# A vision block on one core: layer norm writes the padded layout, clearings move to the start, VectorE masks the turned keys, the last q and k pair is projected behind the first scores

## The chip, the cores and the metric

The kernel runs on one NeuronCore of a Trainium2 chip. The metric is the device time of one launch in microseconds (us). The engines are TensorE (PE, its weight loads PEld), VectorE (DVE), ScalarE (ACT), GpSimd (POOL) and SyncE (SP), which here issues the DMAs. Each runs its own instructions in order; semaphores join them.

## The reference

16 images of 36 patches and a class token (S = 37 rows of D = 256) go through quantised patch embedding, attention and an expert layer:

```
h = tok(x)                       # rms norm, 8-bit activations, ternary weights, + class token, position
h = h + attn(layernorm(h))
h = h + ffn(layernorm(h))

# attn: 16 heads of 16; q_rot, k_rot are q, k turned by position
num  = exp(q_rot @ k_rot^T * scale)
den  = sum(exp(q @ k^T * scale))          # of the unturned q, k
attn = where(causal, num / den, 0)
y    = (attn @ v) @ Wout + bout
# ffn: softmax attention in 8 heads of 64, values and outputs through the expert that the gate picks
```

## The kernel before, in words

**Embedding.** Rows come in six groups (`G`) of three images (111 rows; the sixth group has one image). Each group is squared and rounded by ScalarE, scaled and clipped by VectorE, turned and multiplied by TensorE. GpSimd computes `rrms`, a power of -1/2, from ScalarE's sums. The ternary weights come from `tw`, whose absolute sum VectorE takes (L864) once its DMA has landed.

**First layer norm.** `embed(g)` and `ln_stats` on VectorE, `rstd_of` on GpSimd, `ln_apply` on VectorE (L836, writes `xhat`), `turn_x` on TensorE (L1175). ScalarE's `x1_hi` (L562) then takes the high part of the turned group from PSUM, and VectorE's `x1_lo` (L852) the rest: each fp32 product is made of three matmuls on such halves (`split3`, L267 to L269). Both write tokens without gaps, `x1hi` and `x1lo` [128, 2, 666].

**Projections.** `PJ` lists twelve jobs, in pairs: q and k of images 0 to 7 for each of two chunks of 128 columns (jobs 0 to 3), v of images 0 to 7 (4, 5), q and k of images 8 to 15, chunk 0 (6, 7), v of the others (8, 9), q and k of images 8 to 15, chunk 1 (10, 11). A q or k job is 6 matmuls of 296 columns, a v job 12 of 256. `PJB` names each job's PSUM bank; `bank_free` waits until ScalarE, and for q and k VectorE, have read the job that last used it. The v jobs take their stationary operand from a second, padded copy, 64 columns an image, whose 27 spare columns are zero: `x1hi2`, `x1lo2`, written by ScalarE in `x1_apart` (L638, four instructions).

**Reads of the projections.** ScalarE copies each q or k job twice under a mask of heads (L587, `qun`, `kun`) and each v job in four pieces into `vblk` (L596). VectorE's `rope(r)`, r = 0 to 3, turns a q and k pair in five steps (L922 to L925, then two masked copies L927 into `qrot`); ScalarE's `keys_turned(r)` (L663) writes the turned keys into `krot` with two masked copies. `rope_t` counts VectorE's steps, `krot_ready` ScalarE's. GpSimd clears `vblk` and the spare columns of `kun` and `krot` behind the last `rstd_of` (L467, L469), then adds a bias to `h` (L472) once `x1lo` is complete.

**Attention.** Four blocks (`b`) of four images. On TensorE: `scores(b, 0)` (turned), `denominators(b - 1)`, `scores(b, 1)` (unturned), `attend(b)`; scores are L1254, `attend` L1272, denominators L1284. ScalarE takes the exponentials (L654), VectorE applies the causal mask (L934, `causal`), the reciprocal and the product (L948, L953). Then come the output projection (L1297), the second layer norm, gates, value experts and output experts, which the change does not touch. The order on every engine is that in which its code is written.

## Time and profile before

| what | us |
|---|---|
| median of 3 runs | 263.17 |
| lowest, highest | 259.93, 264.06 |
| time of the profiled execution | 263.35 |
| its span | 260.8 |
| TensorE busy | 222.7 (85%) |
| VectorE busy | 181.9 (70%) |
| ScalarE busy | 99.8 (38%) |
| GpSimd busy | 79.1 (30%) |

The span runs from the first to the last instruction; 2.55 us of the execution's time lie around it. The busy shares are averages over stages with different limits: TensorE's 40 slices are full (8 or 9 tenths) in most of the span, and emptiest in the first 11 and around the fifteenth to seventeenth. The granted clock of TensorE, in the line PEclk, stands at half its full 2.4 GHz in some slices between 39 and 98 us. The stretch of the change ends where attention is in its regular step, at about 69 us.

### The profile page before, as it was taken

How to read it: one execution, taken by the hardware profiler on the slowest of the kernel's cores; microseconds unless marked ns; L12 is line 12 of the kernel's file. 1: busy time of each engine (PE TensorE's matmuls, PEld its weight loads, DVE VectorE, ACT ScalarE, POOL GpSimd, SP SyncE). 2: the span in 40 equal slices, each digit the busy share in tenths (PEclk: the TensorE clock that was granted, in tenths of full speed). 3: DMA queues.
4: the chain of work that ended last, by engine and by line, in shares of the span. 5: the costliest groups of instructions: out<-in, count | busy, mean ns of one | idle time of the engine just before them, and what ended most of it. 6: DMA issues, size and time to landing. Idle time of an engine off the chain costs nothing.

```text
span 260.8 us, 5163 instructions
## 1 busy us (share of the span) xinstructions
PE 222.7 (85%) x2079; PEld 192.4 (74%) x2079; DVE 181.9 (70%) x316; ACT 99.8 (38%) x196; POOL 79.1 (30%) x82
## 2 busy tenths in 40 slices
PE   0146845977899996999999999999999999999994
PEld 0026735966788865899766777777898999999993
DVE  2678995935556268679343766866579997979982
ACT  3677636698544213254444126235520211120000
POOL 4153887200023205240031653775666000000000
PEclk9999995696555579799999999999999999999999
DMA  6995000000000000200034100604700542461102
GB/s 183 252 324 218 1 3 0 1 0 3 3 3 0 3 3 0 80 4 0 0 96 161 64 21 1 230 14 148 200 3 26 188 152 86 154 188 48 48 0 94
DMA packets 7181, 19.56 MB, mean 75 GB/s; under 512 B 1043, under 2 KB 1878, under 8 KB 7030
## 3 DMA queue, kind: packets, MB, share of 16 engines
q1 hardware_dynamic: 7158, 19.24, 23.0%
q8 instruction: 16, 0.26, 0.4%
q14 instruction: 7, 0.06, 0.1%
HBM read 18.55 MB, written 0.68 MB: 74 GB/s over the span
## 4 chain that ended last, share of the span: by engine, by line
PE 48%; DVE 27%; ACT 9%; issue 8%; POOL 4%; DMA 3%; SPq 0%; DVEq 0%; ACTq 0%; POOLq 0%
PE ps L267 10%; PE ps L269 9%; PE ps L268 9%; DVE gx L1119 7%; PE ps L1254 7%; DMA tw<-tok_weight 3%; DVE xhat L836 3%; PE ps L1297 3%; ACT vblk L596 2%; PE ps L1454 2%; DVE oelo L1093 2%; PE ps L1272 1%; DVE amax L796 1%; DVE stat L825 1%; PE ps L1284 1%
## 5 line engine op out<-in xcount | busy, mean ns | idle before, releaser
L1119 DVE TENSOR_TENSOR gx<-maskb,oT 128x1184 fp32r<-128x1184 bf16 x31 | 42.3, 1411 | 0.6 <-PE ps L269 0.5
L267 PE MATMUL ps<-gx,oelo 128*128 128x296 f32 x124 | 37.8, 304 | 0.6 <-DVE gx L1119 0.6
L1056 DVE COPY_PREDICATED v<-onehot,ps 128x512 f32<-128x512 uint8 (+3 forms) x40 | 25.7, 660 | 17.6 <-PE ps L269 17.3
L269 PE MATMUL ps<-gx,oehi 128*128 128x296 f32 x124 | 37.2, 300 | 0.0
L268 PE MATMUL ps<-gx,oehi 128*128 128x296 f32 x124 | 37.0, 298 | 0.0
L267 PE MATMUL ps<-vehi,x2lo 128*128 128x512 f32 (+3 forms) x90 | 35.2, 392 | 0.0
L268 PE MATMUL ps<-velo,x2hi 128*128 128x512 f32 (+3 forms) x90 | 33.3, 370 | 0.0
L269 PE MATMUL ps<-vehi,x2hi 128*128 128x512 f32 (+3 forms) x90 | 33.2, 369 | 0.0
L486 POOL TENSOR_TENSOR velo<-veraw,vehi 128x1024 fp32r<-128x1024 f32 x8 | 19.1, 2389 | 23.4 <-ACT vehi L680 17.3
L267 PEld LDWEIGHTS ps<-gx,oelo 128*128 128x128 f32 x124 | 23.3, 188 | 1.8 <-issue 1.4
L268 PEld LDWEIGHTS ps<-gx,oehi 128*128 128x128 f32 x124 | 23.4, 188 | 0.0
L269 PEld LDWEIGHTS ps<-gx,oehi 128*128 128x128 f32 x124 | 23.3, 188 | 0.0
L1155 PE MATMUL ps<-ident_bf,qb 111*128 111x111 bf16 x36 | 4.5, 297 | 17.4 <-DVE qb L821 17.3
L267 PEld LDWEIGHTS ps<-vehi,x2lo 128*128 128x128 f32 (+1 forms) x90 | 16.2, 180 | 4.2 <-issue 0.7
L269 PEld LDWEIGHTS ps<-vehi,x2hi 128*128 128x128 f32 (+1 forms) x90 | 16.2, 180 | 3.7
L268 PEld LDWEIGHTS ps<-velo,x2hi 128*128 128x128 f32 (+1 forms) x90 | 16.2, 181 | 2.8
L1155 PEld LDWEIGHTS ps<-ident_bf,qb 111*128 111x128 bf16 x36 | 3.1, 139 | 19.3 <-DVE qb L821 19.2
L750 ACT ACTIVATE oehi<-oeraw 128x1024 fp32r<-128x1024 f32 x8 | 8.5, 1065 | 18.8 <-DMA oeraw<-output_w 18.8
L449 POOL TENSOR_TENSOR w2lo<-w2raw,w2hi 128x544 fp32r<-128x544 f32 x4 | 5.3, 1333 | 34.1 <-DVE en L934 33.1
L1254 PE MATMUL ps<-qrot,krot 64*101 64x74 f32 x128 | 12.0, 379 | 3.3 <-ACT vblk L596 3.3
L454 POOL TENSOR_TENSOR rstd<-lnv,half_neg 111x1 f32<-111x1 f32 x12 | 7.9, 658 | 22.9 <-DVE lnv L827 22.8
L1254 PEld LDWEIGHTS ps<-qrot,krot 64*101 64x101 f32 x128 | 11.2, 285 | 3.8 <-issue 3.6
(167 smaller groups left out, 508.4 us busy)
## 6 DMA issues: line engine op xcount, KB each, us to landing
maskb<-mask_rows SPq DMA_DIRECT2D x32, 148.0 KB, 3.7
veraw<-value_w SPq DMA_DIRECT2D x8, 512.0 KB, 3.8
oeraw<-output_w SPq DMA_DIRECT2D x8, 512.0 KB, 3.6
...
```

What stands on the lines that cost most here:

```text
L267: pe.matmul(o, llo, rhi, start=start, stop=False)
L268: pe.matmul(o, lhi, rlo, start=False, stop=False)
L269: return pe.matmul(o, lhi, rhi, start=False, stop=stop)
L454: pool.tensor_tensor(rstd[:, which, g:g + 1], lnv[:, which, g:g + 1], half_neg[0:R, 0:1], ALU.pow).then_inc(sm["rstd_ready"], 1)
L486: pool.tensor_tensor(velo[:, e % NVR], veraw[:, e % NVR], vehi[:, e % NVR].bitcast(F32), ALU.subtract).then_inc(sm["velo_ready"], 1)
L750: act.activation(oehi[u % NOR][:], oeraw[RAW[u]][:], ACT.Copy).then_inc(sm["oehi_ready"], 1)
L836: dve.tensor_scalar(xhat[:, g % 2], h[:, g], mv[:, which, g, 0:1], rstd[:, which, g:g + 1], ALU.subtract, ALU.mult).then_inc(sm["xhat_read ...
L1056: dve.copy_predicated(v2[0:m, t, h0:h1], bcast(onehot[0:m, t, h0:h1, e], 2, DH2), ps[0:m, JBANK[n], 0:(h1 - h0) * DH2].rearrange("p (a b) ...
L1119: dve.tensor_tensor(gx[:, k % NGR].rearrange("p a b t -> p a (b t)"), bcast(maskb[:, w % NMR, k % MEU], 1, 2), oT[:, c % 2].bitcast(F32), ...
L1155: ins = pe.transpose(dst[:, c * (R + 1):c * (R + 1) + R], qb[:, g % NQB, c * P:(c + 1) * P], ident_bf[0:R, 0:R])
L1254: ins = pe.matmul(ps[0:QR, 2 * t + r, o:o + JS * S], key, qry, start=True, stop=True)
L1297: ins = pe.matmul(ps[0:R, o, w:w + D], yT[:, k, g * R:(g + 1) * R], wo[:, k], start=(k == 0), stop=(k == KC - 1))
```

## The change

There is no second copy of x1: ScalarE and VectorE write `x1hi` and `x1lo` in the padded layout [128, 2, 16, 64], and the q and k jobs read 38 columns of each image (`SE`, of which the last is a cleared one), so 304 columns a matmul instead of 296. `x1_apart` is gone. The clearings of `vblk` and `kun` stand first on GpSimd, that of `krot` and of `ones` behind group 0's `rrms`, those of `x1hi` and `x1lo` behind group 1's; `vblk`, `kun`, `krot` and the exponentials get memory that no earlier buffer uses. VectorE writes `krot` itself, two instructions more in each `rope` (`RSTEPS` 8), and `keys_turned` is gone. Jobs 10 and 11, their reads on ScalarE and `rope(3)` on VectorE move behind the first scores, and the v jobs 8 and 9 use banks 4 and 5.

```diff
 NPATCH = SIDE * SIDE
...
 HALF = T // 2
+QH = B // 2 * SE
...
-        x1hi = sbuf(proj, "x1hi", [P, KC, TP], F32R, "right")
-        x1lo = sbuf(proj, "x1lo", [P, KC, TP], F32R, "right")
-        x1hi2 = sbuf(proj, "x1hi2", [P, KC, B, DH2], F32R, "right")
-        x1lo2 = sbuf(proj, "x1lo2", [P, KC, B, DH2], F32R, "right")
+        x1hi = sbuf(proj, "x1hi", [P, KC, B, DH2], F32R, "right")
+        x1lo = sbuf(proj, "x1lo", [P, KC, B, DH2], F32R, "right")
         wo = sbuf(first, "wo", [P, KC, D])
         biasb = sbuf(first, "biasb", [R, 2, D])
+        kun = sbuf(first, "kun", [P, KC, B, QR])
+        krot = sbuf(first, "krot", [P, KC, B, QR])
+        w2raw = sbuf(first, "w2raw", [P, KC, W2C])
+        vblk = sbuf(first, "vblk", [QR, B, PAIRS, 2, DH1])
...
+        ropet = sbuf(first, "ropet", [P, 2, 2, QH])
+        ropex = sbuf(first, "ropex", [P, 2, QH])
+        partner = sbuf(first, "partner", [P, 2, QH])
...
+        rden = sbuf(proj, "rden", [P, UN * S], F32, "right")
+        yT = sbuf(proj, "yT", [P, KC, TP], F32, "right")
+        en = sbuf(proj, "en", [QR, 2, 2, RT, KC, 2, JS, S], F32, "right")
+        ed = sbuf(proj, "ed", [QR, RT, KC, BI, JS, S], F32, "right")
...
-        PJB = [0, 1] + [2, 3] + [4, 5] + [6, 7] + [0, 1] + [4, 5]
+        PJB = [0, 1] + [2, 3] + [4, 5] + [6, 7] + [4, 5] + [6, 7]
         PJPREV = [max([m for m in range(n) if PJB[m] == PJB[n]], default=-1) for n in range(NPJ)]
-        RSTEPS = 6
+        RSTEPS = 8
...
-            pool.memset(ones[:], 1.0).then_inc(sm["pool_setup"], 1)
             pool.memset(half_neg[:], -0.5).then_inc(sm["pool_setup"], 1)
-            for apart in (x1hi2, x1lo2):
-                pool.memset(apart[:, :, :, S:].bitcast(F32), 0.0).then_inc(sm["apart_zero"], 1)
-            pool.wait_ge(sm["pool_setup"], 2)
+            pool.memset(vblk[:].rearrange("p i h a b -> p (i h a b)"), 0.0).then_inc(sm["vblk_zero"], 1)
+            pool.memset(kun[:, :, :, S:DH2], 0.0).then_inc(sm["keys_zero"], 1)
+            pool.wait_ge(sm["pool_setup"], 1)
 
...
+                if g == 0:
+                    pool.memset(krot[:, :, :, S:DH2], 0.0).then_inc(sm["keys_zero"], 1)
+                    pool.memset(ones[:], 1.0).then_inc(sm["pool_setup"], 1)
+                elif g == 1:
+                    for apart in (x1hi, x1lo):
+                        pool.memset(apart[:, :, :, S:].bitcast(F32), 0.0).then_inc(sm["apart_zero"], 1)
...
-            pool.wait_ge(sm["wqlo_ready"], NW)
-            pool.memset(vblk[:].rearrange("p i h a b -> p (i h a b)"), 0.0).then_inc(sm["vblk_zero"], 1)
-            for keys in (kun, krot):
-                pool.memset(keys[:, :, :, S:DH2], 0.0).then_inc(sm["keys_zero"], 1)
             pool.wait_ge(sm["x1lo_ready"], G)
...
-                act.activation(x1hi[:, :, g * R:(g + 1) * R],
-                               ps[:, 4 + g % 2, 0:KC * R].rearrange("p (c t) -> p c t", c=KC),
+                n = images(g)
+                act.activation(x1hi[:, :, g * GI:g * GI + n, 0:S],
+                               ps[:, 4 + g % 2, 0:KC * R].rearrange("p (c i s) -> p c i s", c=KC, s=S)[:, :, 0:n],
                                ACT.Copy).then_inc(sm["x1hi_ready"], 1)
...
-                    src = ps[:, PJB[n], 0:HALF].rearrange("p (i s) -> p i s", s=S)
+                    src = ps[:, PJB[n], 0:QH].rearrange("p (i s) -> p i s", s=SE)[:, :, 0:S]
...
-            def x1_apart(hf):
-                tc, im = slice(hf * HALF, (hf + 1) * HALF), slice(hf * B // 2, (hf + 1) * B // 2)
-                for once, apart in ((x1hi, x1hi2), (x1lo, x1lo2)):
-                    src = once[:, :, tc].bitcast(F32).rearrange("p c (i s) -> p c i s", s=S)
-                    act.activation(apart[:, :, im, 0:S], src, ACT.Copy).then_inc(sm["x1_apart"], 1)
...
-            def keys_turned(r):
-
-                hf, c = r // KC, r % KC
-                act.wait_ge(sm["keys_zero"], 2)
-                act.wait_ge(sm["rope_t"], RSTEPS * r + 4)
-                src = ropet[:, r % 2, 1].rearrange("p (i s) -> p i s", s=S)
-                for j in range(2):
-                    ins = act.activation(krot[:, c, hf * B // 2:(hf + 1) * B // 2, DH2 * j:DH2 * j + S], src, ACT.Copy,
-                                         scale=cols("par")[:, j:j + 1])
-                ins.then_inc(sm["krot_ready"], 1)
-
-            for n in range(NPJ):
+            for n in range(NPJ - 2):
                 proj_read(n)
-                if n == 2:
-                    x1_apart(0)
-                elif n == 4:
-                    x1_apart(1)
-                elif n in (5, 7, 9):
-                    keys_turned((n - 5) // 2)
...
-                    keys_turned(3)
+                    proj_read(NPJ - 2)
+                    proj_read(NPJ - 1)
...
-                tc = slice(g * R, (g + 1) * R)
-                dve.tensor_tensor(x1lo[:, :, tc], ps[:, 4 + g % 2, 0:KC * R].rearrange("p (c t) -> p c t", c=KC),
-                                  x1hi[:, :, tc].bitcast(F32), ALU.subtract).then_inc(sm["x1lo_ready"], 1)
+                n = images(g)
+                hi, lo = (x[:, :, g * GI:g * GI + n, 0:S] for x in (x1hi, x1lo))
+                dve.tensor_tensor(lo, ps[:, 4 + g % 2, 0:KC * R].rearrange("p (c i s) -> p c i s", c=KC, s=S)[:, :, 0:n],
+                                  hi.bitcast(F32), ALU.subtract).then_inc(sm["x1lo_ready"], 1)
...
-                own = ps[:, PJB[n]:PJB[n] + 2, 0:HALF]
+                own = ps[:, PJB[n]:PJB[n] + 2, 0:QH]
...
-                if r >= 2:
-                    dve.wait_ge(sm["krot_ready"], r - 1)
...
-                    many(dve.tensor_scalar(qrot[:, c, im, j], ropet[:, r % 2, 0].rearrange("p (i s) -> p i s", s=S),
-                                           cols("par")[:, 4 + j:5 + j], None, ALU.mult))
+                    many(dve.tensor_scalar(qrot[:, c, im, j], tmp[:, 0], cols("par")[:, 4 + j:5 + j], None, ALU.mult))
+                for j in range(2):
+                    many(dve.tensor_scalar(krot[:, c, im, DH2 * j:DH2 * j + S], tmp[:, 1], cols("par")[:, j:j + 1],
+                                           None, ALU.mult))
...
-            for r in range(2 * KC):
-                rope(r)
+            rope(0)
+            dve.wait_ge(sm["keys_zero"], 2)
+            rope(1)
+            rope(2)
             causal(0)
+            rope(3)
...
-                        wb, tc, col = kind, slice(a * HALF, (a + 1) * HALF), slice(c * P, (c + 1) * P)
-                        ins = split3(pe, ps[:, PJB[n], 0:HALF], wqhi[:, wb, k, col], wqlo[:, wb, k, col],
-                                     x1hi[:, k, tc], x1lo[:, k, tc], k == 0, k == KC - 1)
+                        wb, im, col = kind, slice(a * B // 2, (a + 1) * B // 2), slice(c * P, (c + 1) * P)
+                        ins = split3(pe, ps[:, PJB[n], 0:QH].rearrange("p (i s) -> p i s", s=SE),
+                                     wqhi[:, wb, k, col], wqlo[:, wb, k, col],
+                                     x1hi[:, k, im, 0:SE], x1lo[:, k, im, 0:SE], k == 0, k == KC - 1)
                 else:
                     pe.wait_ge(sm["apart_zero"], 2)
-                    pe.wait_ge(sm["x1_apart"], 2 * (a * NVI * 2 // B + 1))
...
-            for n in range(NSTART, NPJ):
+            for n in range(NSTART, NPJ - 2):
...
-                pe.wait_ge(sm["krot_ready"], KC * late)
                 pe.wait_ge(sm["act_read"], act_reads(PJ.index(("qk", late - 1, KC - 1, 1))))
                 if b == kind == 0:
-                    for n in range(NPJ):
-                        if PJB[n] < 4 and n not in PJPREV:
-                            bank_free(n)
+                    bank_free(NEARLY - 1)
...
+                    bank_free(NPJ - 3 if b == 0 else NPJ - 1)
...
             for b in range(NB):
                 scores(b, 0)
-                if b:
+                if b == 0:
+                    proj_job(NPJ - 2)
+                    proj_job(NPJ - 1)
+                else:
                     denominators(b - 1)
                 scores(b, 1)
```

TensorE, end of the projections and start of attention, before (the last nine matmuls of jobs 10 and 11, then scores(0, 0), scores(0, 1) and attend(0)):

```order
L267 MATMUL ps<-x1hi,wqlo 128x296
L268 MATMUL ps<-x1lo,wqhi 128x296
L269 MATMUL ps<-x1hi,wqhi 128x296
L267 MATMUL ps<-x1hi,wqlo 128x296
L268 MATMUL ps<-x1lo,wqhi 128x296
L269 MATMUL ps<-x1hi,wqhi 128x296
L267 MATMUL ps<-x1hi,wqlo 128x296
L268 MATMUL ps<-x1lo,wqhi 128x296
L269 MATMUL ps<-x1hi,wqhi 128x296
L1254 MATMUL ps<-qrot,krot 101x74 x16
L1254 MATMUL ps<-qun,kun 101x74 x16
L1272 MATMUL ps<-en,vblk 32x37 x32
```

The same place in the change (L1233 is `scores`, L1250 `attend`; the three rows ahead end job 9):

```order
L265 MATMUL ps<-wqhi,x1lo 101x256
L266 MATMUL ps<-wqlo,x1hi 101x256
L267 MATMUL ps<-wqhi,x1hi 101x256
L1233 MATMUL ps<-qrot,krot 101x74 x16
L265 MATMUL ps<-x1hi,wqlo 128x304
L266 MATMUL ps<-x1lo,wqhi 128x304
L267 MATMUL ps<-x1hi,wqhi 128x304
L265 MATMUL ps<-x1hi,wqlo 128x304
L266 MATMUL ps<-x1lo,wqhi 128x304
```

The twelve matmuls of jobs 10 and 11 now stand between scores(0, 0) and scores(0, 1).

VectorE, before: `rope(2)` from its first row, `rope(3)`, then the causal mask of block 0.

```order
L922 STREAM_SHUFFLE partner<-ps 128x592
L923 TENSOR_TENSOR ropet<-ps,cst 128x592
L924 TENSOR_TENSOR ropex<-partner,cst 128x592
L925 TENSOR_TENSOR ropet<-ropet,ropex 128x592
L927 TENSOR_SCALAR qrot<-ropet,cst 128x8x37 x2
L922 STREAM_SHUFFLE partner<-ps 128x592
L923 TENSOR_TENSOR ropet<-ps,cst 128x592
L924 TENSOR_TENSOR ropex<-partner,cst 128x592
L925 TENSOR_TENSOR ropet<-ropet,ropex 128x592
L927 TENSOR_SCALAR qrot<-ropet,cst 128x8x37 x2
L934 TENSOR_TENSOR en<-en,cst 101x592 x2
```

In the change `rope(2)` ends with two copies into `krot`, the mask comes next and `rope(3)` behind it:

```order
L899 STREAM_SHUFFLE partner<-ps 128x608
L900 TENSOR_TENSOR ropet<-ps,cst 128x16x37
L901 TENSOR_TENSOR ropex<-partner,cst 128x16x37
L902 TENSOR_TENSOR ropet<-ropet,ropex 128x16x37
L904 TENSOR_SCALAR qrot<-ropet,cst 128x8x37 x2
L906 TENSOR_SCALAR krot<-ropet,cst 128x8x37 x2
L913 TENSOR_TENSOR en<-en,cst 101x592 x2
L899 STREAM_SHUFFLE partner<-ps 128x608
L900 TENSOR_TENSOR ropet<-ps,cst 128x16x37
L901 TENSOR_TENSOR ropex<-partner,cst 128x16x37
L902 TENSOR_TENSOR ropet<-ropet,ropex 128x16x37
```

ScalarE, reads of jobs 2 to 7 before (L638 is `x1_apart`, L663 `keys_turned`):

```order
L587 ACTIVATE qun<-ps,cst 128x8x37 x2
L638 ACTIVATE x1hi<-x1hi 128x2x8x37
L638 ACTIVATE x1lo<-x1lo 128x2x8x37
L587 ACTIVATE kun<-ps,cst 128x8x37 x2
L596 ACTIVATE vblk<-ps 37x2x8x16 x4
L638 ACTIVATE x1hi<-x1hi 128x2x8x37
L638 ACTIVATE x1lo<-x1lo 128x2x8x37
L596 ACTIVATE vblk<-ps 37x2x8x16 x4
L663 ACTIVATE krot<-ropet,cst 128x8x37 x2
L587 ACTIVATE qun<-ps,cst 128x8x37 x2
L587 ACTIVATE kun<-ps,cst 128x8x37 x2
L663 ACTIVATE krot<-ropet,cst 128x8x37 x2
```

The same reads in the change, and those of jobs 8 to 11 around the exponentials:

```order
L587 ACTIVATE qun<-ps,cst 128x8x37 x2
L587 ACTIVATE kun<-ps,cst 128x8x37 x2
L596 ACTIVATE vblk<-ps 37x2x8x16 x8
L587 ACTIVATE qun<-ps,cst 128x8x37 x2
L587 ACTIVATE kun<-ps,cst 128x8x37 x2
L596 ACTIVATE vblk<-ps 37x2x8x16 x8
L648 ACTIVATE en<-ps 101x592 x2
L587 ACTIVATE qun<-ps,cst 128x8x37 x2
L587 ACTIVATE kun<-ps,cst 128x8x37 x2
L648 ACTIVATE ed<-ps 101x4x148 x2
```

Four copies of x1 and the copies of turned keys are gone from ScalarE, and the reads of jobs 10 and 11 stand behind the exponentials of scores(0, 0).

## Rows read from the trace of the kernel before

**Rows 1.** Page, part 2: TensorE's granted clock in 40 slices of 6.5 us

```profile
PEclk9999995696555579799999999999999999999999
```

**Rows 2.** Chain that ended last, in order of time, 40 to 61 us: start us, us, what

```profile
40.90 0.65 PE ps L1175 x2
...
45.46 0.60 ACT x1lo L638
...
60.18 0.98 ACT krot L663 x2
```

**Rows 3.** Timeline of GpSimd: start us, us, engine line op out<-in, count [idle before <-releaser]

```profile
27.93 1.27 POOL L432 TENSOR_TENSOR wqlo<-wqraw,wqhi 128x512 fp32r<-128x512 f32 x1
...
35.64 3.51 POOL L467 MEMSET vblk<- 101x4096 f32 x1
...
39.87 0.83 POOL L469 MEMSET krot<- 128x864 f32 x1
42.43 2.81 POOL L472 TENSOR_TENSOR h<-h,biasb 111x256 f32<-111x256 f32 x4 [1.73 <-DVE x1lo L852]
```

**Rows 4.** Timeline of VectorE, 9 to 68 us

```profile
9.45 0.22 DVE L809 TENSOR_SCALAR amc<-amax,rrms 111x1 f32<-111x1 f32 x1 [1.18 <-POOL rrms L440]
...
10.67 1.75 DVE L864 TENSOR_REDUCE small<-tw 128x1 f32<-128x1536 f32 x1 [0.61 <-DMA tw<-tok_weight]
...
28.96 0.15 DVE L827 TENSOR_SCALAR lnv<-mv 111x1 f32<-111x1 f32 x1
...
34.87 0.41 DVE L836 TENSOR_SCALAR xhat<-h,mv,rstd 111x256 f32<-111x256 f32 x1
...
35.73 5.12 DVE L836 TENSOR_SCALAR xhat<-h,mv,rstd 111x256 f32<-111x256 f32 x1
...
44.11 0.82 DVE L922 STREAM_SHUFFLE partner<-ps 128x592 f32<-128x592 f32 x1
...
48.39 0.81 DVE L922 STREAM_SHUFFLE partner<-ps 128x592 f32<-128x592 f32 x1
...
62.93 0.82 DVE L922 STREAM_SHUFFLE partner<-ps 128x592 f32<-128x592 f32 x1
...
66.05 0.66 DVE L927 TENSOR_SCALAR qrot<-ropet,cst 128x296 f32<-128x296 f32 x2
66.63 1.45 DVE L934 TENSOR_TENSOR en<-en,cst 101x592 f32<-101x592 f32 x2
```

**Rows 5.** Timeline of ScalarE, 42 to 51 us

```profile
42.37 0.90 ACT L587 ACTIVATE qun<-ps,cst 128x296 f32<-128x296 f32 x2
...
49.09 1.55 ACT L596 ACTIVATE vblk<-ps 37x256 f32<-37x256 f32 x4 [2.25 <-PE ps L269]
```

**Rows 6.** Timeline of TensorE, 36 to 96 us

```profile
36.28 0.30 PE L269 MATMUL ps<-x1hi,wqhi 128*128 128x296 f32 x1
...
41.21 0.60 PE L267 MATMUL ps<-x1hi,wqlo 128*128 128x296 f32 x1
...
44.07 0.45 PE L269 MATMUL ps<-x1hi,wqhi 128*128 128x296 f32 x1
...
52.35 0.28 PE L267 MATMUL ps<-wqhi,x1lo 128*101 128x256 f32 x1
...
55.15 0.30 PE L267 MATMUL ps<-x1hi,wqlo 128*128 128x296 f32 x1
...
60.30 3.00 PE L1254 MATMUL ps<-qrot,krot 64*101 64x74 f32 x32 [3.35 <-ACT vblk L596]
...
68.79 3.00 PE L1254 MATMUL ps<-qrot,krot 64*101 64x74 f32 x32
...
76.93 3.00 PE L1254 MATMUL ps<-qrot,krot 64*101 64x74 f32 x32
...
92.09 3.02 PE L1297 MATMUL ps<-wo,yT 128*111 128x256 f32 x8
```

**Rows 7.** Busy time by stretch: us, busy of each engine, granted clock, DMA share, GB/s

```profile
94.00:96.00 2.00, 2.00 (x15) 1.02 (x14) 0.82 (x2) 0.00 (x0) 0.00 (x0) 0.94 0.00 0
```

More of the change, by code:

```diff
@@ L21 @@
 S = NPATCH + 1
+SE = S + S % 2
 D = 256
@@ L172, in vit_block @@
         tok.close()
-        ropet = sbuf(first, "ropet", [P, 2, 2, HALF])
-        ropex = sbuf(first, "ropex", [P, 2, HALF])
-        partner = sbuf(first, "partner", [P, 2, HALF])
+        ropet = sbuf(first, "ropet", [P, 2, 2, QH])
+        ropex = sbuf(first, "ropex", [P, 2, QH])
+        partner = sbuf(first, "partner", [P, 2, QH])
         qun = sbuf(first, "qun", [P, KC, B, JS, S])
-        kun = sbuf(first, "kun", [P, KC, B, QR])
         qrot = sbuf(first, "qrot", [P, KC, B, JS, S])
-        krot = sbuf(first, "krot", [P, KC, B, QR])
-        vblk = sbuf(first, "vblk", [QR, B, PAIRS, 2, DH1])
-        w2raw = sbuf(first, "w2raw", [P, KC, W2C])
+        rden = sbuf(proj, "rden", [P, UN * S], F32, "right")
+        yT = sbuf(proj, "yT", [P, KC, TP], F32, "right")
+        en = sbuf(proj, "en", [QR, 2, 2, RT, KC, 2, JS, S], F32, "right")
+        ed = sbuf(proj, "ed", [QR, RT, KC, BI, JS, S], F32, "right")
         proj.close()
-        soft = ExitStack()
-        en = sbuf(soft, "en", [QR, 2, 2, RT, KC, 2, JS, S], F32, "right")
-        ed = sbuf(soft, "ed", [QR, RT, KC, BI, JS, S], F32, "right")
-        rden = sbuf(soft, "rden", [P, UN * S], F32, "right")
-        yT = sbuf(soft, "yT", [P, KC, TP], F32, "right")
-        soft.close()
         first.close()
@@ L250, in vit_block @@
             qpar dqs_ready amaxed yround_ready qb_ready qT_ps proj_ps h0_ready lnv_ready rstd_ready xhat_ready x1T_ps x1hi_ready
-            x1lo_ready x1_apart apart_zero keys_zero vblk_zero wqhi_ready wqlo_ready w2hi_ready w2lo_ready act_read rope_t krot_ready proj1_ps qT2_sb
+            x1lo_ready apart_zero keys_zero vblk_zero wqhi_ready wqlo_ready w2hi_ready w2lo_ready act_read rope_t proj1_ps qT2_sb
             s_ps exp_ready en_ready pv_ps den_ps rden_ready yT_ready yT_pad op_ps h0b_ready h1_ready x2T_ps x2hi_ready
@@ L908, in by_image @@
                 def by_image(a):
-                    return a.rearrange("p k (i s) -> p k i s", s=S)
+                    return a.rearrange("p k (i s) -> p k i s", s=SE)[:, :, :, 0:S]
                 def many(ins):
@@ L1210, in proj_job @@
                         for k in range(KC):
-                            xh, xl = (x[:, k, i:i + 2].rearrange("p i s -> p (i s)")[:, 0:QR] for x in (x1hi2, x1lo2))
+                            xh, xl = (x[:, k, i:i + 2].rearrange("p i s -> p (i s)")[:, 0:QR] for x in (x1hi, x1lo))
                             ins = split3(pe, ps[0:QR, PJB[n], ii * D:(ii + 1) * D], xh, xl,
@@ L1258, in attend @@
                 if b < 2:
-                    pe.wait_ge(sm["act_read"], act_reads(NPJ - 1))
-                    pe.wait_ge(sm["rope_t"], rope_reads(NPJ - 1))
+                    bank_free(NPJ - 3 if b == 0 else NPJ - 1)
                 if b >= 2:
@@ L1278, in denominators @@
                 if b < 2:
-                    pe.wait_ge(sm["act_read"], act_reads(NPJ - 1))
-                    pe.wait_ge(sm["rope_t"], rope_reads(NPJ - 1))
+                    bank_free(NPJ - 3 if b == 0 else NPJ - 1)
                 if b >= 2:
```

## The prediction

> **What bounds the kernel now.** I read the granted clock first, then the chain of waits, then the timelines engine by engine from 27 to 77 us. Ahead of 35 us and behind 69 us nothing is rewritten but the clearings, so the question is how much earlier the regular step of attention starts.
>
> The chain enters the stretch with an oddity. The sixth `xhat` takes 5.12 us, its twin just ahead 0.41 [rows 4]. Over the same time GpSimd runs three clearings, from 35.64 to 40.70 [rows 3]; `xhat` ends at 40.85. I read that as VectorE held out of SBUF by GpSimd. TensorE had issued its last matmul of job 1 at 36.28 and turns this `xhat` at 40.90 [rows 2, 6], and by 41.21 its granted clock has fallen: twelve matmuls start from 41.21 to 44.07, 0.25 us apart once the first is out, at 1.2 GHz, against (55.15 - 52.35) / 24 = 0.117 us for the v matmuls at 2.4 GHz [rows 6].
>
> From there the chain is ScalarE: the copies of x1 end at 46.06, then reads of v, turned keys and reads of q and k up to 61 us [rows 2]. TensorE waits 3.35 us for the last `vblk` before scores(0, 0) at 60.30 [rows 6]. Then attention goes in regular blocks, 68.79 to 76.93, 8.14 us each, with TensorE almost without gaps at 1.2 GHz [rows 1, 6].
>
> **The clearings.** The stall goes: `xhat` ends near 36.14 (35.73 + 0.41). TensorE is next late: the turn is queued behind job 1 and starts near 36.45 instead of 40.90, a gain of **4.45 us**. TensorE then has work until about 46 us: jobs 2, 3, 6 and 7 at about 0.14 us a matmul (a little over half the cold 0.25, and 304 columns for 296) 3.4 us, four v jobs 2 x 2.8 = 5.6 [rows 6], so no fall of the clock in there. The reads of job 1 end at 44.11 now [rows 4] and at **39.6** then; that is when `rope(0)` can start. The gain does not need `x1_apart` to be gone.
>
> At the start GpSimd's clearings take 3.51 + 0.83 us from about 0.8 us and end near 5.1, when ScalarE's first sum, GpSimd's first input, is due as well. Behind group 1's `rrms` lie 2 x 0.83 = 1.66 us, from 9.4 to 11.1. VectorE's tiny operations of that moment start at 9.45 [rows 4]. Similar tiny ones ran in 0.15 us at 28.96 while GpSimd was subtracting from 27.93 to 29.20 [rows 3, 4], so I take them as not held up. VectorE then waits 0.61 us for `tw` anyway [rows 4]. Cost 0; bounds 0 and 1.0 (all held until 11.1, 0.6 us of them, then L864 at 11.7 instead of 10.67).
>
> The Trainium skill (SBUF — State Buffer, "SBUF: two separate sides") says that GpSimd and VectorE share a port pair under a lock held for the whole instruction, against a VectorE operation in a 2-port mode or with two SBUF inputs. The 5.12 us agree. Read strictly it speaks against the new places: the scales of group 1 could be held until 11.1, which makes the sum 1.0 us worse; the row at 28.96 speaks for my reading.
>
> **VectorE's new path.** A `rope` takes 66.63 - 62.93 = 3.70 us alone and 48.39 - 44.11 = 4.28 beside GpSimd's additions to `h` [rows 3, 4]. Those additions move from 42.43 to near 37.8; six at 0.7 us and more end near 42.4, so they still touch `rope(0)`. Each `rope` gains two masked copies; the two of `qrot` take 0.66 [rows 4], with ScalarE's 0.98 for the turned keys [rows 2] as the upper bound; I take 0.66 and 0.02 for the wider shuffle. `rope(0)` and `rope(1)`: 4.28 + 3.70 + 2 x 0.68 = 9.34, so 39.6 + 9.34 = **48.95** is when scores(0, 0) can start, instead of 60.30.
>
> That VectorE is last there must hold against the others. TensorE ends job 9 at 45.9; its job 8 needs the bank of job 4. ScalarE reads a q or k job in 0.8 us and a v job in 1.55 [rows 5]: from 37.9 (42.37 less the 4.45) it has six and four, 11.0 us, done near 48.9, and it is needed for exponentials from 50.4 on. Its four copies of x1 (2.8 us) and six of keys (2.9) ahead of scores cost nothing any more. So scores start **11.35 us** earlier.
>
> **The last pair.** Between scores(0, 0) and scores(0, 1) TensorE now has jobs 10 and 11: 12 x 0.25 = 3.0 us at 1.2 GHz. They need banks 6 and 7, free after the second step of `rope(2)` near 50.6, before the scores end at 51.9: no wait. Their reads on ScalarE end at 55.8, before the exponentials of scores(0, 1) are due. VectorE masks block 0 at 53.3 to 54.8 (`rope(2)` ends at 53.3), `attend(0)` starts after 57.8. `rope(3)` runs from 55.8 to 60.2; attend(1) and block 2 need it at 66 and 67. The start of scores(0, 0) to that of scores(1, 0) is 68.79 - 60.30 = 8.49 us now, 7.3 of it TensorE's work [rows 6]. Then: 3.0 + 3.0 + 3.0 + 1.2 = 10.15. Loss **1.7 us**. Block 1 starts at 59.1 instead of 68.79.
>
> **Sum.** 11.35 - 1.7 = **9.65 us** less, all of it handed on, since everything behind keeps its order and its needs: w2's low halves wait for masks, the loads for halves already in SBUF. The profiled execution took 263.35 (span 260.8, 2.55 around it), so 253.7; it lies 0.18 above the median, so 253.5 against 263.17.
>
> **The clock.** TensorE is idle for 3.05 us ahead of scores(0, 0), 45.9 to 48.95, as long as it was ahead of 60.30 (3.35, to 60.30), where the clock fell. So I start attention at 1.2 GHz. But the 3.0 us of dense projections lie inside it now. Before, the scores never brought the clock up, while 2 us of output projection (from 92.09) did, at about 94.1 [rows 6, 7]. Some stretch at 2.4 GHz behind jobs 10 and 11 is likely; it can save up to half of a scores and an attend, 2.1 us, and I take 1.0. **Forecast 252.5 us.**
>
> **Rivals.**
>
> *The clock stays up through attention.* If dense jobs 10 and 11 raise it, or the gap ahead of them doesn't let it fall, and the scores hold it, a block shrinks from 8.14 towards 4.07, where VectorE's and ScalarE's shares of a block (two masks 1.45, the reciprocal and the exponentials) come to bound it. Over three blocks at most 12.2, more like 8: 245, with 241 as the floor. For it: from 94 us on TensorE held 2.4 GHz for some microseconds with denominators and an attend in them [rows 1, 7]. Against: 23 us of scores at nearly full occupation did not raise it. The Trainium skill (TensorE: Matmul & The Clock Gate, "The HAM clock gate") says that the throttle is the default and activity releases it; by that rule the inserted jobs would raise the clock. Whether scores then keep it no row shows. Chance 0.15.
>
> *VectorE's path is dearer.* If the copies into `krot` and GpSimd's additions get in each other's way (2.8 us of additions lie beside `rope(0)`, and 0.58 is counted) and a copy pair costs nearer 0.98, scores start 1 to 4 us later: 254.5 to 257.5, typically 256. The startup loss of 1.0 belongs here. Chance 0.16.
>
> *The clearings are not what stalls `xhat`.* Then 4.45 are lost: 257. The match of the ends (40.70 and 40.85) speaks against. Chance 0.03.
>
> *Slower: the padded operand.* TensorE may stream the q and k columns, 38 of every 64, below full rate. If they ran like plain fp32, which takes 3.02 / 4 / 256 = 2.95 ns a column at 1.2 GHz in the output projection against 0.25 / 296 = 0.84 for a split half [rows 6], 3.5 times: the 36 matmuls ahead of scores cost 2.5 x 0.14 x 36 = 12.6 more, of which 3.05 fill idle time, and the last pair 2.5 x 3.0 = 7.5. Net 17.1 - 9.65: 270.5. The sign turns at 2.6 times. Against: nothing in the matmul but the access pattern changes, and the v jobs' operands already come from the padded copy at 0.117 us. Chance 0.03.
>
> **How the numbers follow.** The forecast has 0.63, over 250.5 to 254.5 (clock term 0 to 2.1, start-up and copies a little either way, runs that scattered by 4 us). The range 246 to 257 leaves out half of the first rival, the tail of the second and the padded operand, about 0.17. A difference of 2% is 5.3 us, about what a measurement of this kernel tells from no change: faster means below 257.9, slower above 268.4. Faster gets the forecast, the first rival and most of the second and third: 0.93; within 2% 0.05; slower 0.02.
>
> **What would show it.** Right: no `xhat` over 1 us; the sixth turn near 36.5; no wait of TensorE until about 46; `rope(0)` at 39.6, each `rope` 4.4 to 5 us; scores(0, 0) near 49, released by VectorE; jobs 10 and 11 without a gap; scores(1, 0) near 59; the same tail. Wrong: q and k matmuls much over 0.14 us at 2.4 GHz, a long VectorE row at 5 or 9.5 us, `rope(0)` over 6 us, TensorE's blocks unlike 8.14 us, or time given back behind 100 us, where the clock dips once more [rows 1] and a shift of 10 us may move the dip.

## The result and the profile after

| | before | changed |
|---|---|---|
| median, us | 262.55 (4 runs, 259.93 to 264.06) | **240.64** (4 runs, 239.21 to 241.91) |
| profiled execution, us | 263.35 | 240.91 |
| its span, us | 260.8 | 238.4 |
| mean granted clock of TensorE | 0.908 | 0.979 |

The changed kernel takes 0.9195 of the time before (95% interval 0.9098 to 0.9291), 22 us less. The forecast was 252.5 with a range of 246 to 257: the direction was right, the size wrong by 12 us. The executions of one kernel can be of two kinds, by the clock that TensorE got: of the 21 executions of the kernel before that ran beside the experiments, 19 took 259.98 to 264.24 us at a mean clock of 0.89 to 0.92, one 255.85 (0.929) and one 256.39 (0.935).

The page of the changed kernel: busy us (share of the span) x instructions, and the granted clock in 40 slices of 6 us.

```profile
span 238.4 us, 5151 instructions
...
PE 207.9 (87%) x2079; PEld 179.6 (75%) x2079; DVE 178.7 (75%) x324; ACT 93.7 (39%) x184; POOL 79.5 (33%) x82
...
PEclk9999999979999679999999999999999999999999
```

The fives and sixes of before [rows 1], seven slices, are gone; what is left is a 7 in the ninth slice and a 6 and a 7 in the fourteenth and fifteenth. Nearly the same matmuls keep TensorE busy for 15 us less (222.7 before). The timeline of TensorE in the changed kernel shows where (L1157 turns `xhat`, L265 to L267 are the projections, L1233 is `scores`, L1250 `attend`, L1261 the denominators, L1274 the output projection; columns as in rows 3):

```profile
36.28 0.36 PE L1157 MATMUL ps<-cst,xhat 111*128 111x111 f32 x2
...
45.57 0.28 PE L267 MATMUL ps<-wqhi,x1hi 128*101 128x256 f32 x1
48.30 2.47 PE L1233 MATMUL ps<-qrot,krot 64*101 64x74 f32 x32 [2.45 <-issue]
50.70 0.62 PE L265 MATMUL ps<-x1hi,wqlo 128*128 128x304 f32 x1
...
53.12 0.30 PE L267 MATMUL ps<-x1hi,wqhi 128*128 128x304 f32 x1
53.35 1.65 PE L1233 MATMUL ps<-qun,kun 64*101 64x74 f32 x32
54.93 0.78 PE L1250 MATMUL ps<-en,vblk 101*32 101x37 f32 x64
55.66 1.65 PE L1233 MATMUL ps<-qrot,krot 64*101 64x74 f32 x32
...
59.72 1.07 PE L1250 MATMUL ps<-en,vblk 101*32 101x37 f32 x64 [0.17 <-DVE en L913]
60.71 1.65 PE L1233 MATMUL ps<-qrot,krot 64*101 64x74 f32 x32
...
65.34 1.65 PE L1233 MATMUL ps<-qrot,krot 64*101 64x74 f32 x32
...
70.44 1.95 PE L1274 MATMUL ps<-wo,yT 128*111 128x256 f32 x8 [1.21 <-DVE yT L935]
...
81.90 3.73 PE L1274 MATMUL ps<-wo,yT 128*111 128x256 f32 x8 [0.75 <-DVE yT L935]
```

The landmark of before that answers to the last of these rows, from TensorE's timeline of the kernel before:

```profile
104.62 3.56 PE L1297 MATMUL ps<-wo,yT 128*111 128x256 f32 x8 [1.35 <-DVE yT L953]
```

The spans between the same landmarks, before [rows 6] and after:

| stretch | before | after | difference | forecast |
|---|---|---|---|---|
| start to scores(0, 0) | 60.30 | 48.30 | -12.0 | -11.35 |
| to scores(1, 0) | 8.49 | 7.36 | -1.1 | +1.7 |
| to the first output projection | 23.30 | 14.78 | -8.5 | 0 |
| to the last in attention's tail | 12.53 | 11.46 | -1.1 | 0 |
| to the end | 156.2 | 156.5 | +0.3 | 0 |

The forecast's 1.0 us for the clock is in none of these rows; it was to come somewhere behind jobs 10 and 11.

Everything ahead of attention came within 0.7 us of the forecast. A block of attention, 8.14 us before, takes 60.71 - 55.66 = 5.05 and 65.34 - 60.71 = 4.63: 32 scores take 1.65 us, not 3.00. That is the clock. The windows of the changed kernel (busy us and instructions of PE, PEld, DVE, ACT, POOL; then the granted clock, the DMA share, GB/s):

```profile
46.00:48.00 2.00, 0.00 (x0) 0.00 (x0) 1.93 (x6) 1.93 (x6) 0.00 (x0) 1.00 0.00 0
48.00:50.00 2.00, 1.70 (x27) 1.73 (x28) 1.97 (x5) 0.88 (x2) 0.00 (x0) 0.73 0.00 0
50.00:52.00 2.00, 2.00 (x15) 1.87 (x13) 1.93 (x5) 0.77 (x2) 0.00 (x0) 0.50 0.03 8
52.00:54.00 2.00, 2.00 (x23) 1.82 (x23) 1.87 (x4) 1.42 (x4) 0.00 (x0) 0.91 0.00 0
54.00:56.00 2.00, 2.00 (x96) 1.88 (x93) 1.55 (x4) 1.95 (x4) 0.00 (x0) 1.00 0.00 0
...
80.00:82.00 2.00, 1.25 (x6) 0.92 (x5) 1.97 (x3) 0.42 (x1) 1.78 (x1) 0.50 0.00 0
```

The idle time ahead of scores(0, 0) does cost the clock, as forecast, during its scores (0.73, then 0.50). It is back at 2.4 GHz from about 52.2 us, with jobs 10 and 11 half done, and **stays there through all of attention**, until about 80.

### The profile page after: what moved, and what is told of

It is laid out like the page before. It is cut to its first block, busy times and chain, and to the rows that moved or that the text cites. A ratio compares the mean times of both kernels' runs of the same rounds, so it can differ in the third digit from the quotient of the medians.

```text
span 238.4 us, 5151 instructions
## 1 busy us (share of the span) xinstructions
PE 207.9 (87%) x2079; PEld 179.6 (75%) x2079; DVE 178.7 (75%) x324; ACT 93.7 (39%) x184; POOL 79.5 (33%) x82
## 4 chain that ended last, share of the span: by engine, by line
PE 49%; DVE 28%; issue 9%; ACT 4%; POOL 4%; DMA 4%; SPq 1%; DVEq 0%; ACTq 0%; POOLq 0%
PE ps L265 13%; PE ps L266 11%; PE ps L267 11%; DVE gx L1101 7%; DMA tw<-tok_weight 4%; PE ps L1233 3%; PE ps L1274 2%; PE ps L1434 2%; DVE oelo L1075 2%; DVE rden L930 2%; DVE amax L774 1%; PE ps L1404 1%; ACT ptb L720 1%; DVE stat L803 1%; POOL velo L485 1%
## 5 line engine op out<-in xcount | busy, mean ns | idle before, releaser
L265 PE MATMUL ps<-gx,oelo 128*128 128x296 f32 x124 | 37.8, 305 | 0.6 <-DVE gx L1101 0.6
L267 PE MATMUL ps<-gx,oehi 128*128 128x296 f32 x124 | 37.2, 300 | 0.0
L265 PE MATMUL ps<-vehi,x2lo 128*128 128x512 f32 (+3 forms) x90 | 35.2, 392 | 0.0
L267 PE MATMUL ps<-vehi,x2hi 128*128 128x512 f32 (+3 forms) x90 | 33.2, 369 | 0.0
L265 PEld LDWEIGHTS ps<-gx,oelo 128*128 128x128 f32 x124 | 23.3, 188 | 1.8 <-issue 1.3
L267 PEld LDWEIGHTS ps<-gx,oehi 128*128 128x128 f32 x124 | 23.3, 188 | 0.0
L265 PEld LDWEIGHTS ps<-vehi,x2lo 128*128 128x128 f32 (+1 forms) x90 | 16.2, 180 | 4.2 <-issue 0.7
L267 PEld LDWEIGHTS ps<-vehi,x2hi 128*128 128x128 f32 (+1 forms) x90 | 16.2, 180 | 3.7
L707 ACT ACTIVATE pe<-sc 101x444 f32<-101x444 f32 (+1 forms) x6 | 3.2, 534 | 24.5 <-POOL sc L500 24.5
L265 PE MATMUL ps<-x2hi,w2lo 128*128 128x296 f32 x32 | 11.0, 345 | 0.1
```

Source lines behind the costliest of these rows:

```text
L265: pe.matmul(o, llo, rhi, start=start, stop=False)
L267: return pe.matmul(o, lhi, rhi, start=False, stop=stop)
```

## Experiments

Theory A: the two dense jobs inside attention raise the clock, and attention, which by itself seldom raises it, then holds it. Where an expectation uses letters, A is this theory, and another letter is the rival that the same text describes. Before ran beside them, seven times each: 260.98 (255.85 to 262.42) beside the dense jobs cut down, the clock kept up, the dense matmuls in the kernel before and the clearings back; 260.8 (260.04 to 264.24) beside the early clearings alone, the keys on ScalarE, the second copy and the two holes both filled; 261.15 (256.39 to 263.93) beside the half dose, each hole filled alone and the changed kernel again.

**The dense jobs cut down.** The changed kernel with one matmul instead of six in each of jobs 10 and 11, so the q and k of the last pair are wrong and ten matmuls of work are gone.

```diff
+ if n >= NPJ - 2:
+     if k == 0:
+         ins = pe.matmul(o, wqhi[:, wb, k, col], x1hi[:, k, im, 0:SE], start=True, stop=True)
+     continue
  ins = split3(pe, o, ...
```

> The changed kernel with one matmul in place of six in each of jobs 10 and 11 (q and k of images 8 to 15, chunk 1 are not computed fully), so that some 0.5 us instead of 3 us of dense matmuls stand between scores(0, 0) and scores(0, 1). Theory A (the dense matmuls bring TensorE's granted clock to 2.4 GHz, and attention keeps it there): without them attention runs at 1.2 GHz, blocks of 8.1 us instead of 4.6 to 5.1, and the time is 240.6 - 2.3 (matmuls left out) + 10 to 12 = 248 to 251 although there is less work. Theory B (the clock comes up for another reason: less idle time, the fast jobs ahead of scores): it still rises within 4 us of the first scores, and the time is 238 to 240.

Measured: **250.27** (249.85 to 251.49). Its clock line, and its TensorE timeline (L1188 are the two matmuls left, L1238 scores):

```profile
PEclk9999999955555979999999999999999999999999
```

```profile
49.65 0.87 PE L1188 MATMUL ps<-x1hi,wqhi 128*128 128x304 f32 x2
...
54.53 3.00 PE L1238 MATMUL ps<-qrot,krot 64*101 64x74 f32 x32
...
62.67 3.00 PE L1238 MATMUL ps<-qrot,krot 64*101 64x74 f32 x32
```

Less work, and 9.6 us slower than the changed kernel. The blocks are again 62.67 - 54.53 = 8.14 us, as before. VectorE's masks, the early clearings and the missing copies are all still in this kernel, so none of them brings the clock back. Put the ten matmuls back at 0.25 us each and it would take 252.8, an estimate: the forecast's 252.5 is this kernel, whose clock never comes up before the output projection.

**Half the dose.** Three matmuls instead of six in each of the two jobs (the contraction over the second 128 features is left out).

```diff
+ if n >= NPJ - 2 and k:
+     continue
```

> The changed kernel with three matmuls in place of six in each of jobs 10 and 11 (the second chunk of the contraction is left out), 1.5 us of dense matmuls between the scores, half of the change's and three times that of e1_no_dense. Theory A says that the clock comes up if the dense share is large enough: either 238 to 240 (it suffices) or 249 to 251 (it does not), or executions of both kinds; each of these is a reading of how near the change is to the edge. Only a time between, 243 to 246, in every execution would speak against a clock with two levels that attention holds.

Measured: 251.71, 249.89, 240.38, 239.83, 238.68. Two kinds, nothing between, at mean clocks of 0.917 and 0.931 and of 0.978 to 0.991. The profiled one is the first; TensorE's timeline there (L1235 scores):

```profile
51.81 0.46 PE L267 MATMUL ps<-x1hi,wqhi 128*128 128x304 f32 x1
52.20 3.00 PE L1235 MATMUL ps<-qun,kun 64*101 64x74 f32 x32
...
56.27 3.00 PE L1235 MATMUL ps<-qrot,krot 64*101 64x74 f32 x32
```

So 1.8 us of dense matmuls (50.38 to 52.20) raised the clock or not, from execution to execution; 2.65 us (50.70 to 53.35 in the changed kernel) did in each of its eight timed executions, 239.21 to 241.91.

**The clock kept up ahead of attention, the dense jobs cut down.** As the first experiment, but with twenty matmuls of no use in the idle time ahead of scores(0, 0).

```diff
  if b == kind == 0:
+     bank_free(1)
+     pe.wait_ge(sm["w2hi_ready"], 4)
+     for j in range(20):
+         pe.matmul(ps[:, 0, 0:256], w2hi[:, 0, 0:P], w2hi[:, 1, 0:256], start=True, stop=True)
...
+     pe.wait_ge(sm["rope_t"], RSTEPS * KC * late)      # the wait for VectorE, now behind the twenty
```

> As e1_no_dense (jobs 10 and 11 of one matmul each), and 20 extra dense matmuls of 256 columns into a free bank fill TensorE's idle stretch ahead of scores(0, 0), so that it enters attention at 2.4 GHz; no dense block lies inside attention. Theory A (attention holds a clock that it can't raise): 2.4 GHz from 36 to beyond 70 us, scores(0, 0) in 1.6 us, time 237 to 240. Rival (attention at 2.4 GHz needs the dense block inside, or falls by itself in a few us): the clock falls during block 0 or 1, and the time is 245 to 250, near e1_no_dense.

Measured: 246.85, 239.22, 245.29, 241.06, 240.18. Against 250.27 without the twenty, three executions of five bring the whole gain, at mean clocks of 0.977 to 0.984: a clock that is up at the start of attention can be enough. The other two, at 0.944 and 0.951, are what the text calls the rival. In the profiled one, the slowest, it was lost inside (L1261 attend, L1244 scores):

```profile
52.58 1.07 PE L1261 MATMUL ps<-en,vblk 101*32 101x37 f32 x64 [1.26 <-DVE en L913]
53.58 2.20 PE L1244 MATMUL ps<-qrot,krot 64*101 64x74 f32 x32
...
56.85 3.00 PE L1244 MATMUL ps<-qun,kun 64*101 64x74 f32 x32
```

The scores run at 1.65 us up to 51.3; then TensorE waits 1.26 us for the mask of block 0, since only two short matmuls stand where jobs 10 and 11 were, and it runs at 1.2 GHz from within the next scores. So the moved jobs do a second thing: they keep TensorE busy while VectorE turns the keys and masks.

**Dense matmuls in the kernel before.** Twelve matmuls of no use, 296 columns each, between scores(0, 0) and scores(0, 1) of the old kernel. Nothing else is changed.

```diff
  scores(b, 0)
+ if b == 0:
+     bank_free(7)
+     pe.wait_ge(sm["w2hi_ready"], 4)
+     for j in range(12):
+         pe.matmul(ps[:, 6, 0:HALF], w2hi[:, 0, 0:P], w2hi[:, 1, 0:HALF], start=True, stop=True)
```

> The kernel before with 12 extra dense matmuls of 296 columns into a free bank between scores(0, 0) and scores(0, 1), nothing else changed. It is pure extra work of up to 3.0 us. Theory A: they bring the clock up and attention holds it; blocks 1 to 3 take 4.6 to 5.1 us instead of 8.1, and the time falls from 262.5 to 252 to 255. Rival (the clock stays up only in the changed kernel's tighter schedule): 263 to 266, slower by the extra work.

Measured: 247.75, 249.51, 247.13, and 255.84 in the profiled one: median 248.63 against 260.98, better than the 252 to 255 expected. **Useless work made the old kernel faster**, by 12 us at the medians. Against the one execution of before that had the better clock, 255.85, three are still 6.3 to 8.7 us faster and the fourth equals it. This is the clearest test of A, since no other part of the change is there. The profiled execution, TensorE's timeline (L1320 are the twelve, L1272 attend, L1254 scores):

```profile
60.96 1.90 PE L1320 MATMUL ps<-w2hi 128*128 128x296 f32 x12
...
66.63 1.07 PE L1272 MATMUL ps<-en,vblk 101*32 101x37 f32 x64 [2.19 <-DVE en L934]
...
71.13 3.00 PE L1254 MATMUL ps<-qun,kun 64*101 64x74 f32 x32
...
75.20 1.65 PE L1254 MATMUL ps<-qrot,krot 64*101 64x74 f32 x32
```

Here the clock was up, fell after a wait of 2.19 us for VectorE, and came back at about 75 with nothing but scores, denominators and an attend ahead of it. So attention can raise the clock, though in the profiles of before and of the first two experiments it did not. It may do so in the kernel before as well, in the executions of 255.85 and 256.39; neither was profiled. What tips it is open.

**Clearings back at their old place**, in the changed kernel.

```diff
- pool.memset(vblk[:]..., 0.0)      # at the start
+ pool.wait_ge(sm["wqlo_ready"], NW)
+ pool.memset(vblk[:]..., 0.0)      # behind the last rstd; kun and krot too
```

> The changed kernel with the clearings of vblk, kun and krot back behind the last rstd, where they were. If they stall the sixth xhat through GpSimd: that xhat takes 5.1 us again, the turn starts 4.4 us later, TensorE falls to 1.2 GHz at about 40 us but rises by the dense jobs, and the time is 240.6 + 4.4 to 5.5 = 245 to 246. If something else stalled it: 240 to 241.

Measured: 244.32 (243.23 to 245.11), 3.7 us more than the changed kernel and just under the 245 to 246 expected. VectorE, where the clearings run on GpSimd from 34.88 to 39.93, and TensorE:

```profile
34.96 5.12 DVE L815 TENSOR_SCALAR xhat<-h,mv,rstd 111x256 f32<-111x256 f32 x1
```

```profile
40.13 0.63 PE L1158 MATMUL ps<-cst,xhat 111*128 111x111 f32 x2 [4.25 <-DVE xhat L815]
...
52.42 1.65 PE L1234 MATMUL ps<-qrot,krot 64*101 64x74 f32 x32 [0.32 <-issue]
```

`xhat` takes 5.12 us again, the sixth turn waits 4.25 us for it and scores(0, 0) starts 4.12 later. The clearings are the stall.

**Early clearings alone**, in the kernel before, with memory of their own at the start.

```diff
+ kun = sbuf(first, "kun", [P, KC, B, QR])    # and krot, vblk, w2raw
...
+ pool.memset(vblk[:]..., 0.0)                # first on GpSimd; kun, krot, ones, x1hi2, x1lo2 as in the change
```

> The kernel before with only the clearings moved to the start (and vblk, kun, krot in memory of their own). The forecast's term for it was 4.45 us, of ScalarE's chain, with attention still at 1.2 GHz since no dense matmuls lie in it: 256 to 257 against 261. Rival (the clock is carried into attention once TensorE has no stall at 36 to 41 us): 248 to 250.

Measured: 258.19 (254.71 to 258.54) against 260.8; ratio 0.9833 (0.971 to 0.9956), a gain of less than 2%. 256 to 257 was expected. TensorE (L1255 scores, L1298 output projection):

```profile
63.12 3.00 PE L1255 MATMUL ps<-qrot,krot 64*101 64x74 f32 x32
...
71.27 3.00 PE L1255 MATMUL ps<-qrot,krot 64*101 64x74 f32 x32
...
99.54 3.72 PE L1298 MATMUL ps<-wo,yT 128*111 128x256 f32 x8 [0.55 <-DVE yT L954]
```

Attention's blocks are 8.15 us, at 1.2 GHz. scores(1, 0) starts 68.79 - 63.12 = 5.67 us earlier; 104.62 - 99.54 = 5.08 are left at the last projection of attention's tail and 4.1 at the end of the span (256.7 against 260.8). About 1 us is given back in the second dip of the clock, which is longer here: 0.50 to 0.65 from 96 to 104 us, where before has 0.62 and 0.53 from 104 to 108. The medians are only 2.6 apart, since the profiled execution of before, 263.35, lies above its median.

**Turned keys masked by ScalarE again**, in the changed kernel.

```diff
- for j in range(2):                                  # VectorE, rope(r)
-     many(dve.tensor_scalar(krot[...], tmp[:, 1], ...))
+ def keys_turned(r):                                 # ScalarE, behind reads 5, 7, 9 and 11
+     act.wait_ge(sm["rope_t"], RSTEPS * r + 4)
+     act.activation(krot[...], src, ACT.Copy, scale=...)
```

> The changed kernel with the turned keys masked by ScalarE again (keys_turned behind the reads of jobs 5, 7, 9 and 11), VectorE's two copies taken out of each rope. VectorE gains 4 x 0.57 us, ScalarE waits for each rope before it can go on to v and the exponentials. Theory A (attention at 2.4 GHz is bounded by VectorE and ScalarE in block 0, and ScalarE's order matters): first exponentials 1.5 to 2.5 us later, time 241.5 to 243. Rival (VectorE's ropes are the bound and ScalarE has slack): scores(0, 0) 1.1 us earlier and the time 239 to 240.

Measured: **253.91** (252.89 to 254.23), 13 us slower than the changed kernel; my expectation missed. ScalarE and TensorE (L1246 scores):

```profile
56.83 0.98 ACT L656 ACTIVATE krot<-ropet,cst 128x296 f32<-128x296 f32 x2 [3.25 <-DVE ropet L917]
```

```profile
58.50 2.83 PE L1246 MATMUL ps<-qrot,krot 64*101 64x74 f32 x32 [4.28 <-ACT ed L648]
...
62.40 3.00 PE L1246 MATMUL ps<-qun,kun 64*101 64x74 f32 x32
```

scores(0, 0) starts even earlier, at 46.95. But `keys_turned(3)` stands ahead of the exponentials of scores(0, 1), and `rope(3)` now comes behind VectorE's mask: ScalarE waits 3.25 us, TensorE behind it 4.28, and after that wait the clock is down for the rest of attention. I had counted 1.5 to 2.5 us on ScalarE and not what is queued behind its wait. The two masked copies on VectorE cost about 0.6 us per `rope`; they are worth the clock.

**The second copy of x1 back**, with its four copies on ScalarE, written to a free buffer that nothing reads, and the v jobs waiting for them.

```diff
+ act.activation(copy, once[:, :, im, 0:S].bitcast(F32), ACT.Copy).then_inc(sm["x1_apart"], 1)
```

> The changed kernel with the four copies of x1 on ScalarE put back behind the reads of jobs 2 and 4 (written to a free buffer), and the v jobs waiting for them as before. Theory A: scores(0, 0) keeps its start, which VectorE sets; ScalarE's first exponentials come 1.5 to 2.5 us later (2.8 us more work, 1.1 us of slack), and the time is 241.5 to 243, as long as the 3 us in which TensorE waits do not cost the clock. Rival (removing x1_apart is what moved attention forward): 4 us or more, 245 and above.

Measured: 241.86 (240.91 to 243.16), ratio to before 0.9256 (0.9175 to 0.9337); the changed kernel's interval overlaps it. TensorE, at the first v job and at scores (L1242):

```profile
41.30 0.33 PE L265 MATMUL ps<-wqhi,x1lo 128*101 128x256 f32 x1 [2.75 <-ACT vehi L654]
...
49.20 1.65 PE L1242 MATMUL ps<-qrot,krot 64*101 64x74 f32 x32
```

scores(0, 0) starts at 49.20, not 48.30, but TensorE's idle time has moved ahead of the v jobs, and this time it cost no clock: it had risen at about 36.2, and is 1.00 from 38 to 54 us. scores(1, 0) then comes at 55.68, against 55.66. By the medians, 241.86 and 240.64, the single padded copy is worth 1.2 us, within the scatter; what the copies cost apart from the clock is not shown.

**Filling the two holes that are left.** In the changed kernel the clock is down twice, from scores(0, 0) to job 11 and from 80 to 86. First the twenty matmuls of no use ahead of scores(0, 0); then nineteen around the second layer norm (three ahead of its second turn, two, two, four, and eight ahead of the last output projection), where TensorE waits for VectorE; then both. The changed kernel ran once more beside the first two.

```diff
+ def busy(n):
+     for j in range(n):
+         pe.matmul(ps[:, 1, 0:256], w2hi[:, 0, 0:P], w2hi[:, 1, 0:256], start=True, stop=True)
...
  for kind, n in D_ORDER:
+     busy({("turn", 1): 3, ("turn", 2): 2, ("gate", 0): 2, ("qk", 0): 4, ("out", 4): 8}.get((kind, n), 0))
```

> The changed kernel with only the 20 extra matmuls ahead of scores(0, 0). TensorE enters attention at 2.4 GHz, so scores(0, 0) takes 1.65 us instead of 2.47 and the last pair 1.7 instead of 2.6; VectorE's mask and ropes bound block 0, so little of it is handed on. Theory A: 239 to 240.5. Rival (a warm start makes TensorE wait more inside block 0 and some executions lose the clock, as in e2_fill_no_dense): executions of 245 to 247 among them.

> The changed kernel with only the 19 extra matmuls around the second layer norm (none ahead of scores). Theory A: attention as in the changed kernel (2.4 GHz from about 52 us), the last two output projections in 1.95 us instead of 3.73 and the first projection behind them at 2.4 GHz: 2 to 2.8 us less, 238 to 238.7. Rival (c2_fill_both had its gain from ahead of scores): 240 to 241.

> The changed kernel with extra matmuls that do nothing useful where TensorE idles: 20 of 256 columns ahead of scores(0, 0), and 19 between the transposes, the first gate and the first projection of the second layer norm, ahead of the last two output projections, which ran at 1.2 GHz (3.73 us for 8 records against 1.95 at 2.4). Theory A (an idle stretch costs the clock of what follows): the granted clock stays at 2.4 GHz from 29 us to the end, output projection 1.95 us, time 240.6 - 0.5 to 1 (block 0) - 2 to 2.5 = 237 to 238. Rival (the extra work costs as much as the clock gives): 240 to 242.

> The changed kernel itself, beside the others on the same chip: 239 to 242, with attention at 2.4 GHz from about 52 us in each execution. If the clock's rise hung on where the launch falls, some execution would stand at 248 to 251.

| kernel | median | lowest, highest |
|---|---|---|
| changed, again | 241.14 | 240.23, 241.52 |
| twenty ahead of scores(0, 0) | 239.87 | 239.10, 241.24 |
| nineteen at the second layer norm | 238.60 | 238.02, 239.45 |
| both | **237.37** | 237.24, 238.27 |

With both, the ratio to before is 0.9088 (0.9015 to 0.9162): 3.3 us under the changed kernel's 240.64, and the best kernel of this study. The first alone is within the scatter. The second alone lies wholly below the changed kernel that ran beside it, though not below the 239.21 of its first runs; the version with both lies below all eight of its executions. For that version, the clock line and TensorE's timeline (L1225 the twenty, L1280 the last output projection of attention's tail):

```profile
PEclk9999999999999999999999999999999999999999
```

```profile
44.97 2.55 PE L1225 MATMUL ps<-w2hi 128*128 128x256 f32 x20
...
80.49 1.95 PE L1280 MATMUL ps<-wo,yT 128*111 128x256 f32 x8 [0.17 <-DVE yT L935]
```

The clock never falls, and the projection that took 3.73 us takes 1.95.

## Why the prediction was wrong, step by step

**The clearings: right.** 4.45 us were counted; the sixth turn starts at 36.28 (forecast 36.45, before 40.90), and putting them back costs 3.7. VectorE and GpSimd in the changed kernel:

```profile
9.43 0.21 DVE L787 TENSOR_SCALAR amc<-amax,rrms 111x1 f32<-111x1 f32 x1 [1.19 <-POOL rrms L437]
...
35.51 0.41 DVE L814 TENSOR_SCALAR xhat<-h,mv,rstd 111x256 f32<-111x256 f32 x1
...
39.10 0.86 DVE L899 STREAM_SHUFFLE partner<-ps 128x608 f32<-128x608 f32 x1
...
43.82 0.85 DVE L899 STREAM_SHUFFLE partner<-ps 128x608 f32<-128x608 f32 x1
...
48.12 0.84 DVE L899 STREAM_SHUFFLE partner<-ps 128x608 f32<-128x608 f32 x1
```

```profile
0.76 3.51 POOL L422 MEMSET vblk<- 101x4096 f32 x1
...
9.35 0.82 POOL L443 MEMSET x1hi<- 128x864 f32 x1
...
37.26 4.75 POOL L471 TENSOR_TENSOR h<-h,biasb 111x256 f32<-111x256 f32 x6 [1.79 <-DVE x1lo L831]
```

`xhat` takes 0.41 us, not 5.12. The start-up cost was put at 0, and is: the tiny operation at 9.43 takes 0.21 us with a clearing beside it from 9.35. Both long ones last through three instructions of GpSimd, not one: before, `xhat` starts at 35.73, 0.09 us behind the first clearing, and ends at 40.85, behind the third [rows 3, 4].

**VectorE's path to scores(0, 0): right.** `rope(0)` starts at 39.10 (forecast 39.6) and the two ropes take 4.72 and 4.30 us, 9.02 for 9.34. TensorE is free from 45.85 (forecast 45.9) and starts scores at 48.30 (48.95). The rivals of a dearer VectorE and of a slow padded operand fall: 304 columns with gaps go at (37.68 - 36.94) / 5 = 0.148 us a matmul, forecast 0.14. (The price of the padded operand's rival was misread: 3.02 us for the projection at 92.09 is not 1.2 GHz throughout, since the clock rose at about 94 [rows 6, 7]; at 1.2 GHz it takes 3.73, so plain fp32 would be 4.3 times a split half and not 3.5.)

**The last pair: mechanism right, size wrong by the clock.** 10.15 us were counted from scores(0, 0) to scores(1, 0); it is 7.36: scores 2.40, the pair 2.65, scores 1.58, attend 0.73, against 3.0, 3.0, 3.0 and 1.2. No wait anywhere in it, as forecast.

**"The clock": the step that failed.** The text said "Some stretch at 2.4 GHz behind jobs 10 and 11 is likely", and took 1.0 us for it. The rise was right and came at about 52.2. But a rise is worth a block only if what follows lets the clock fall again, and 8.5 us in blocks 1 to 3, 2.8 in block 0 and 1.1 in the tail came from its not falling. The cut-down kernel, 252.8 with its ten matmuls put back, against 240.64 gives this term 12 us in place of 1.0. It was the first rival, at a chance of 0.15. Its 8 us for blocks 1 to 3 are close to the 8.5 measured, but it left out block 0 and the tail, so the time came out at its floor of 241 and not at its 245.

What misled me is the row "23 us of scores at nearly full occupation did not raise it" [rows 1, 6], which I set against the rival. It shows that attention did not *raise* the clock in that execution. Whether it *holds* it is another question, and the only row on that, 2.4 GHz from 94 us on with denominators and an attend in it [rows 1, 7], spoke for holding. The evidence against was evidence on something else. The Trainium skill (TensorE: Matmul & The Clock Gate, "The HAM clock gate") says that activity releases a throttle that is the default: the dense pair agrees, the 23 us of attention before do not, if a full timeline is taken as activity.

**The rest**: 156.2 us behind attention's tail became 156.5, so all of it was handed on, and the shift of 22 us moved the second dip of the clock (80 to 86) without making it cost more.

**What is shown and what is not.** Shown: without the dense pair the clock stays down with everything else of the change in place; dense matmuls alone bring the old kernel from 260.98 to 248.63; half of the dense pair brings the clock up in three executions of five; waits of 2.19 and 4.28 us inside attention are followed by 1.2 GHz, and so was one of 1.26. Not settled: why 1.26 us cost the clock there while waits of 1.21 us (70.44 above) did not here, nor one of 2.75 us ahead of the v jobs with the second copy back, so that the length of a wait alone does not decide it; and what let the clock come back unaided at 75 us in one execution.
